# Residual as a fourth filter of the strip product, in a graph-attention and expert block on one core

## The reference

```python
out = 0
for k in range(3):                       # three graph filters
    r = einsum('mn,bmn,bmft->bnft', cheb[k], S, x)
    out = out + einsum('bnft,fo->bnot', r, Theta[k])
sg = relu(out)
tc = conv along t (3 taps, tw)(sg) + tb
res = einsum('bnft,of->bnot', x, rw) + rb
y = relu(res + tc)
y = layer_norm_over_t(y) * gamma + beta
```

## Time and profile before

| | |
|---|---|
| timed runs | 947.37, 949.14, 950.04 us (median 949.14) |
| span of the profiled execution | 943.2 us |
| median less span | 5.9 us |
| TensorE busy | 896.8 us, 95% |
| VectorE, ScalarE, GpSimd busy | 604.5, 426.2, 210.3 us |
| steady part | about 240 to 840 us |

### The profile page before, as it was taken

The page is one execution under the profiler, slowest core; times in us unless marked ns, Lnnn a source line. Parts: engine busy times, 40 slices in busy tenths (PEclk is TensorE's granted clock), DMA queues, the critical chain, the costliest instruction groups (busy, mean ns, idle before and its releaser), DMA issues.

```text
span 943.2 us, 19688 instructions
## 1 busy us (share of the span) xinstructions
PE 896.8 (95%) x8000; PEld 799.1 (85%) x8000; DVE 604.5 (64%) x1615; ACT 426.2 (45%) x781; POOL 210.3 (22%) x183
## 2 busy tenths in 40 slices
PE   4898879999999999999999999999999999999997
PEld 3687658998988998898988989888888898988997
DVE  6637967677775379654786458853787537764522
ACT  2534534831674336552464425652366424622442
POOL 2004101233301142112411124021331123122232
PEclk9999999999999999999999999999999999999998
DMA  6000400111011100210002010020001100020121
GB/s 233 2 1 1 171 23 2 57 62 35 13 39 57 35 24 13 73 35 23 24 14 82 24 35 23 25 72 31 27 13 52 55 2 24 30 77 24 38 66 34
DMA packets 36249, 39.26 MB, mean 42 GB/s; under 512 B 3392, under 2 KB 32576, under 8 KB 36160
## 3 DMA queue, kind: packets, MB, share of 16 engines
q1 hardware_dynamic: 36160, 38.01, 12.7%
HBM read 33.02 MB, written 4.98 MB: 40 GB/s over the span
## 4 chain that ended last, share of the span: by engine, by line
PE 85%; DVE 6%; DMA 4%; ACT 2%; issue 2%; POOL 1%; SPq 0%; POOLq 0%; DVEq 0%
PE ring L1355 9%; PE d_ps L521 5%; PE g_ps L521 5%; PE d_ps L522 4%; PE d_ps L523 4%; PE g_ps L523 4%; PE g_ps L522 4%; PE u_ps L522 4%; PE u_ps L521 4%; PE u_ps L523 4%; PE ring L1223 4%; PE num L1252 3%; PE ring L1338 3%; PE ring L1455 3%; PE ring L521 3%; PE ring L523 2%
## 5 line engine op out<-in xcount | busy, mean ns | idle before, releaser
L699 POOL TENSOR_TENSOR hl<-hb,hh 128x512 fp32r<-128x512 f32 x96 | 126.7, 1320 | 480.0 <-ACT hh L836 480.0
L836 ACT ACTIVATE hh<-hb 128x512 fp32r<-128x512 f32 x96 | 60.6, 632 | 181.8 <-DVE hb L1195 169.4
L521 PE MATMUL d_ps<-hh,down_h 128*128 128x256 f32 x384 | 114.9, 299 | 5.1 <-POOL hl L699 5.1
L521 PE MATMUL g_ps<-normed_h,gate_h 128*128 128x256 f32 x352 | 107.4, 305 | 3.5 <-DVE hb L1190 3.5
L1190 DVE TENSOR_TENSOR hb<-sl,u_ps 128x512 f32<-128x512 f32 x88 | 60.2, 684 | 77.2 <-PE u_ps L523 35.9
L522 PE MATMUL d_ps<-hl,down_h 128*128 128x256 f32 x384 | 107.7, 280 | 0.0
L523 PE MATMUL d_ps<-hh,down_l 128*128 128x256 f32 x384 | 107.7, 280 | 0.0
L522 PE MATMUL g_ps<-normed_l,gate_h 128*128 128x256 f32 x352 | 99.8, 283 | 0.0
L523 PE MATMUL g_ps<-normed_h,gate_l 128*128 128x256 f32 x352 | 99.8, 283 | 0.0
L522 PE MATMUL u_ps<-normed_l,up_h 128*128 128x256 f32 x352 | 99.5, 283 | 0.0
L521 PE MATMUL u_ps<-normed_h,up_h 128*128 128x256 f32 x352 | 99.4, 283 | 0.0
(11 more groups left out here) (413 smaller groups left out, 2092.5 us busy)
## 6 DMA issues: line engine op xcount, KB each, us to landing
weights_over_hidden<-weights_by_expert SPq DMA_DIRECT2D x128, 128.0 KB, 2.9
shared<-denominators_by_head SPq DMA_DIRECT2D x16, 256.0 KB
out_x<-kept SPq DMA_DIRECT2D x16, 256.0 KB, 2.2
x_s<-in_x SPq DMA_DIRECT2D x12, 256.0 KB, 3.6
raw_weights<-in_gateT SPq DMA_DIRECT2D x4, 384.0 KB, 6.6
raw_weights<-in_upT SPq DMA_DIRECT2D x4, 384.0 KB, 6.0
raw_weights<-in_down SPq DMA_DIRECT2D x4, 384.0 KB, 8.0
cheb_s<-in_cheb SPq DMA_DIRECT2D x3, 256.0 KB, 4.9
```

What stands on the lines that cost most here:

```text
L521: eng.matmul(ps, wh, xh, start=start, stop=False, **how)
L699: pool.tensor_tensor(hl[:, j % 2, :], hb, hh[:, j % 2, :].bitcast(F32), ALU.subtract).then_inc(*ffn_pool.mark(p, f"lo{j}"))
L836: act.activation(hh[:, j % 2, :], hb, ACT.Copy).then_inc(*ffn_act.mark(p, f"hi{j}"))
```

## The change

The weights of the residual become a fourth filter: `theta_s` gets 4 x 2 x 16 = 128 columns, and TensorE's filter products write whole banks. ScalarE now makes two copies from each of the four banks: the three filters to `y_s` as before, and the fourth to the rows in `kept`, in which it waits for the output store. The bank is free after the second copy. GpSimd then adds the bias to the rows in place. In tc0 and tc1 the bias product and the residual products are gone; TensorE does the temporal convolution alone, VectorE adds the rows to the bank in place, and ScalarE's relu waits for that. The load of `residual_s` and the preparation of `ones`, `bias_h` and `bias_hl` go.

```diff
-        theta_s = sb("theta_s", [P, 3, 2, T])
-        residual_s = sb("residual_s", [P, T, 8])
+        theta_s = sb("theta_s", [P, 4, 2, T])
...
-                READ_OUT[f"Y{b}_{j}"] = [(conv_act, f"y{b}{j}")]
+                READ_OUT[f"Y{b}_{j}"] = [(conv_act, f"r{b}{j}")]
...
+                if name in ("Y0", "Y1"):
+                    b = int(name[1])
+                    if p == 0 and not b:
+                        pool.wait_ge(prep_dve, 6)
+                    pool.wait_ge(conv_act.of(p), conv_act.at(p, f"r{b}3"))
+                    res = x1_at(p)[:, :, b, :].rearrange("p m (c s) -> p m c s", s=2 * T)
+                    pool.tensor_tensor(res, res, bias[:, :, :].rearrange("p t o -> p (t o)").unsqueeze(1).to_broadcast([P, 8, 2 * T]).unsqueeze(1).to_broadcast([P, 2, 8, 2 * T]),
+                                       ALU.add).then_inc(*conv_pool.mark(p, f"rb{b}"))
...
+                    if p >= 3:
+                        act.wait_ge(out_stored[p % 3], 32 * (p // 3))
                     for j, n in enumerate(banks_of(name)):
-                        act.activation(g.y_s[b].rearrange("p m c k s -> p (m c k) s")[:, :, 32 * j:32 * j + 32],
-                                       tile(p, n)[:, 0:384].rearrange("p (q s) -> p q s", s=32), ACT.Copy).then_inc(*conv_act.mark(p, f"y{b}{j}"))
+                        act.activation(g.y_s[b].rearrange("p m c k s -> p (m c) k s")[:, :, :, 32 * j:32 * j + 32],
+                                       tile(p, n)[:, :].rearrange("p (q k s) -> p q k s", k=4, s=32)[:, :, 0:3, :], ACT.Copy).then_inc(*conv_act.mark(p, f"y{b}{j}"))
+                        by_k = tile(p, n)[:, :].rearrange("p (m c k s) -> p m c k s", m=2, c=2, k=4)
+                        act.activation(x1_at(p)[:, :, b, :].rearrange("p m (c s) -> p m c s", c=2)[:, :, :, 32 * j:32 * j + 32], by_k[:, :, :, 3, :],
+                                       ACT.Copy).then_inc(*conv_act.mark(p, f"r{b}{j}"))
...
                 if name in ("tc0", "tc1"):
                     b = int(name[2])
-                    if p >= 3:
-                        act.wait_ge(out_stored[p % 3], 32 * (p // 3))
+                    act.wait_ge(conv_dve.of(p), conv_dve.at(p, f"res{b}"))
...
+                if name in ("tc0", "tc1"):
+                    b = int(name[2])
+                    dve.wait_ge(*filled_at(p, name))
+                    dve.wait_ge(conv_pool.of(p), conv_pool.at(p, f"rb{b}"))
+                    by_o = t[:, :].rearrange("p (m o t) -> p m o t", m=2, t=T)
+                    dve.tensor_tensor(by_o, by_o, x1_at(p)[:, :, b, :].rearrange("p m (t o) -> p m o t", o=T), ALU.add).then_inc(*cv.mark(p, f"res{b}"))
...
-                            last = pe.matmul(tile(p, n)[:, q * 96:(q + 1) * 96], g.xT[rows, b, c, m * P:(m + 1) * P],
+                            last = pe.matmul(tile(p, n)[:, q * P:(q + 1) * P], g.xT[rows, b, c, m * P:(m + 1) * P],
...
-                    pe.matmul(by_o, ones[:, :], bias_hl[:, :].unsqueeze(1).to_broadcast([P, 2, T]).unsqueeze(3).to_broadcast([P, 2, T, T]),
-                              start=True, stop=False, skip_group_check=True)
                     for m in range(2):
                         cols = slice(m * P, (m + 1) * P)
-                        for c in range(2):
-                            pe.matmul(by_o[:, m, :, 8 * c:8 * c + 8], g.xT[:, b, c, cols], residual_s[:, :, :], start=False, stop=False, skip_group_check=True)
-                        pe.matmul(by_o[:, m, :, 0:9], g.sg[:, b, 0, cols], tconv_s[:, :, 1:10], start=False, stop=False, skip_group_check=True)
+                        pe.matmul(by_o[:, m, :, 0:9], g.sg[:, b, 0, cols], tconv_s[:, :, 1:10], start=(m == 0), stop=False, skip_group_check=True)
                         last = pe.matmul(by_o[:, m, :, 7:16], g.sg[:, b, 1, cols], tconv_s[:, :, 0:9], start=False, stop=True, skip_group_check=True)
```

More of the change, by code:

```diff
@@ L217, with graph_attention_moe @@
 PLACE = {f: i for i, f in enumerate(FILLS)}
-def graph_attention_moe(nc, x, out, small, consts, cheb, theta, residual, tconv, vsT, bsT, wqkvT, woT, gateT, upT, down):
+def graph_attention_moe(nc, x, out, small, consts, cheb, theta, tconv, vsT, bsT, wqkvT, woT, gateT, upT, down):
     x_v = x.rearrange("(p b) (c n) f t -> p b n c (f t)", b=2, n=P)
@@ L240, in graph_attention_moe @@
         cheb_s = sb("cheb_s", [P, 3, 2, N])
[L241 to L242 removed]
+        theta_s = sb("theta_s", [P, 4, 2, T])
         tconv_s = sb("tconv_s", [P, T, 10])
[L244 to L246 removed]
+        bias = sb("bias", [P, 2, T])
         vs_s = sb("vs_s", [P, 2, N])
@@ L257, in graph_attention_moe @@
         down_h = sb("down_h", [P, CHUNKS, N], F32R)
-        ones = sb("ones", [P, P], F32R)
         over = sb("weights_over_hidden", [P, 2, 512])
@@ L578, in _ @@
             sp.dma_start(theta_s[:, :, :, :], theta).then_inc(load["blocks"], 16)
-            sp.dma_start(residual_s[:, :, :], residual).then_inc(load["blocks"], 16)
             sp.dma_start(tconv_s[:, :, :], tconv).then_inc(load["blocks"], 16)
@@ L722, in front @@
                 if t is not None:
-                    act_reads = name in ("xT0", "xT1", "lr", "o0", "o1", "tc0", "tc1", "xl0", "xl1", "xn0", "xn1", "kt", "q0", "q1", "k0", "k1", "v0", "v1")
+                    act_reads = name in ("xT0", "xT1", "lr", "o0", "o1", "xl0", "xl1", "xn0", "xn1", "kt", "q0", "q1", "k0", "k1", "v0", "v1")
                     if act_reads:
@@ L726, in front @@
                 if name == "M" and p == 0:
-                    act.wait_ge(prep_dve, 6)
-                    act.wait_ge(prep_pool, 6)
-                    act.activation(bias_h[:, :], bias[:, :], ACT.Copy).then_inc(prep_act, 1)
-                    act.activation(bias_hl[64:65, :], bias[64:65, :], ACT.Copy).then_inc(prep_act, 1)
+                    act.wait_ge(prep_pool, 2)
                 if name in ("xT0", "xT1"):
@@ L851, in prepare @@
                 dve.tensor_tensor(router[:, :, 1, :], small_at("router").rearrange("p (k e) -> p k e", k=2), router[:, :, 0, :].bitcast(F32), ALU.subtract).then_inc(prep_dve, 1)
-                dve.tensor_tensor(bias[:, :], small_at("tb"), small_at("rb"), ALU.add).then_inc(prep_dve, 1)
-                dve.tensor_scalar(ones[:, :], ident, 0.0, 1.0, ALU.mult, ALU.add).then_inc(prep_dve, 1)
+                dve.tensor_tensor(bias[:, :, :], small_at("tb").unsqueeze(1).to_broadcast([P, 2, T]), small_at("rb").unsqueeze(1).to_broadcast([P, 2, T]),
+                                  ALU.add).then_inc(prep_dve, 1)
             def split(i):
@@ L965, in front @@
                     dve.wait_ge(load["rest"], 16)
-                    dve.wait_ge(prep_act, 3)
-                    dve.wait_ge(prep_dve, 6)
-                    dve.tensor_tensor(bias_hl[96:97, :], bias[96:97, :], bias_h[96:97, :].bitcast(F32), ALU.subtract).then_inc(prep_dve, 1)
                     dve.wait_ge(load["graph"], 96)
@@ L1563 @@
     consts = _np.concatenate([c[n].astype(f32) for n in CONST], axis=1)
-    theta = _np.zeros((8, T, 3, 2, T), f32)
-    residual = _np.zeros((8, T, T, 8), f32)
+    theta = _np.zeros((8, T, 4, 2, T), f32)
     tconv = _np.zeros((8, T, T, 10), f32)
     for t in range(8):
-        theta[t, :, :, t % 2, :] = a["L0_conv_Theta"].transpose(1, 0, 2)
-        residual[t, :, :, t] = a["L0_conv_rw"].T
+        theta[t, :, 0:3, t % 2, :] = a["L0_conv_Theta"].transpose(1, 0, 2)
+        theta[t, :, 3, t % 2, :] = a["L0_conv_rw"].T
         tconv[t, :, :, t:t + 3] = a["L0_conv_tw"][:, :, 0, ::-1].transpose(1, 0, 2)
-    theta, residual, tconv = (v.reshape((P,) + v.shape[2:]) for v in (theta, residual, tconv))
+    theta, tconv = (v.reshape((P,) + v.shape[2:]) for v in (theta, tconv))
     given = {
-        "x": a["x"], "small": small, "consts": consts, "cheb": a["L0_conv_cheb"], "theta": theta, "residual": residual, "tconv": tconv,
+        "x": a["x"], "small": small, "consts": consts, "cheb": a["L0_conv_cheb"], "theta": theta, "tconv": tconv,
         "vsT": a["L0_conv_V_s"].T, "bsT": a["L0_conv_b_s"][0].T,
```

19 lines of the change are left out of this document (6 added, 13 removed).

## The result

The changed kernel takes **937.17 us** (median of four runs, 933.71 to 938.39) beside 949.59 for the kernel before, run between them (947.37 to 950.96): a ratio of 0.9869, 95% interval 0.9843 to 0.9896, so it is 12.4 us or 1.3% faster (10 to 15 us). I had forecast 4.9. The direction was right and the range held the time, in part by luck, but the gain is two and a half times the forecast, and the sum behind it has to be taken apart.

A forecast was written before the change was run, and what follows sets the result against it. TensorE, busy 95% of the span, was taken to bound the kernel. Five steady pairs at -0.85 us (-4.2) and the opening (-0.7) gave -4.9, so 949.14 would become 944.3 us; range 935.5 to 952.

The forecast's parts named there:

- Where is this paid?: Places where TensorE feels ScalarE's added copies and the wider products: Y0 0.5 us, Y1 0.35 us a pair.
- 0.5 us behind Y0: Y0: 0.1 wider products plus 0.68 copies less 0.27 slack delay the tanh and the routing weights' copy, per pair.
- 0.35 behind Y1: Y1: ring banks come free later, 0.25 for st1's transposes and 0.1 for o0, per pair.
- a term put at nothing: Behind Y0: the routing weights' DMA chain and TensorE's 0.96 us wait at its end, with only new delay charged.
- tc1 waiting for the relu of o1: At tc1: it would begin at 434.02, just as that relu ends, a new stall of 0.25 us.
- The spacing: ScalarE's four added copies per filter tile start 0.17 us after their neighbours by overlapping: 0.68 us a tile.
- The rivals with full-length copies: Y0 and Y1: each added copy costs its full 0.28 us, 1.1 a tile; 948.0 us, chance 0.22.
- the gate on ScalarE: Y0 and Y1: old copies lose their overlap too, 3.1 us a tile in place of 1.64; 953.6 us, chance 0.13.
- the queue of VectorE ahead of V11 and wo0: After tc: additions delay VectorE's later work; 0.6 us a pair lost, of which 0.25 is tc1's wait for the relu.
- forecast -0.85: Steady part, each pair: -1.7 left of the removed products, +0.5 at Y0, +0.35 at Y1.
- Opening: Pairs 0 to 2, without feed-forward work to hide behind: gains and delays sum to -0.7 us, give or take 1.5.
- The median of the runs lies 5.9 us above the span, which stays: Baseline: median of the runs 5.9 us above the profiled span of 943.2; the gap stays, so 949.14 less 4.9.

The follow-up runs named there:

- experiment 8: Changed kernel without VectorE's addition, ScalarE's residual copies and GpSimd's bias additions; filter products still 128 columns wide, residual and bias missing: 929.98 us, ratio 0.9795.
- experiments 3: Changed kernel without VectorE's addition; the relu reads the bank straight after the convolution, copies and GpSimd's bias additions stay: 929.85 us, ratio 0.9801.
- Experiment 11: Changed kernel with GpSimd writing residual and bias in the bank's order, so VectorE's addition reads 512 numbers in a row: 936.99 us, ratio 0.9863.
- experiment 2: Kernel before with 128 empty waits more at the start of TensorE's stream, moving its instruction loads: 954.93 us, ratio 1.0062.
- experiment 6: Changed kernel with 48 empty waits before TensorE's wait for its first load, on a semaphore up at once: 938.10 us, ratio 0.9889.
- second profiles: Kernel before and changed kernel each run and profiled once more, no edit: 947.64 us (span 945.9) and 936.71 us (span 934.9).
- experiments 1: Kernel before with bias and residual products left out of both temporal convolutions, nothing put in their place: 929.87 us, ratio 0.9794.
- 7: Changed kernel with the old scheme (bias and residual products in tc, three filters, no additions) in pairs 0 and 1: 934.42 us, ratio 0.9846.
- 12: Changed kernel with the old scheme in pairs 0 and 1 and the residual in the bank's order in pairs 2 to 7: 933.59 us, ratio 0.9831.
- 4: Changed kernel with 64 empty waits more at the start of TensorE's stream: 943.15 us, ratio 0.9942.
- 5: Kernel before with 48 empty waits before TensorE's wait for its first load, on a semaphore up at once: 948.78 us, ratio 0.9997.

## Why the prediction was right or wrong

**The step that failed.** The sum missed 7.5 of 12.4 us. Two terms of it were wrong. The first is the answer to "Where is this paid?": I charged the copies and wider products with 0.5 us behind Y0 and 0.35 behind Y1, 0.85 a pair, and TensorE felt 0.25 to 0.3, so nearly 3 us too much in five pairs. The second is a term put at nothing: I took the write of the routing weights, and TensorE's wait at its far end, as given, and looked only at what the change would add to them. In place of that its meetings with instruction loads fell from five to two, 2.3 to 3.9 us. Most of the rest lies at the end of the program (about 1 us) and in how executions differ. (The parts do not add up to 7.5 exactly: the meetings cost other amounts in other executions.) The first term is a mistake about the change; the second is luck, since no part of the edit aims at it.

**What bounds the kernel.** Right: a product removed gave back 94% of its time (2.16 of 2.31 us). I had charged 0.25 us of it for tc1 waiting for the relu of o1. The timeline of after has no such wait, and tc0 to the next step takes 433.56 - 431.66 = 1.90 us where I had 2.2 and before had 4.27 (start, duration, what):

```profile
431.66 0.41 PE L1373 MATMUL ring<-tconv_s,filters 128*128 128x144 f32 x2
431.86 0.60 ACT L775 ACTIVATE filters<-ring 128x512 f32<-128x512 f32 x1 [4.58 <-PE ring L1361]
...
432.64 0.45 PE L1373 MATMUL ring<-tconv_s,filters 128*128 128x144 f32 x2
432.84 2.08 DVE L981 TENSOR_TENSOR ring<-ring,kept 128x512 f32<-128x512 f32 x2 [5.47 <-PE ring L1374]
...
433.56 0.37 PE L517 MATMUL d_ps<-hh,down_h 128*128 128x256 f32 x1
...
433.92 0.60 ACT L779 ACTIVATE kept<-ring 128x512 f32<-128x512 f32 x1 [1.46 <-DVE ring L981]
434.82 1.45 DVE L1005 TENSOR_REDUCE row_sums<-kept 128x32 f32<-128x512 f32 x2
434.95 0.60 ACT L779 ACTIVATE kept<-ring 128x512 f32<-128x512 f32 x1 [0.44 <-DVE ring L981]
```

The convolutions follow each other without a gap; the relu of o1 ends at 432.46, just ahead of tc1. One check in the prediction does not come out: its pieces, 0.41 + 0.31 + 4 x 0.44, make 2.48 and not 2.31 us; the 2.31 from the starts is the better figure.

**ScalarE's copies.** The spacing was right to the hundredth. In after eight copies run from 378.75 to 381.07, 2.32 us against 1.64, so 0.17 for each added one:

```profile
378.75 0.49 ACT L741 ACTIVATE filters<-ring 128x384 f32<-128x384 f32 x1 [1.44 <-issue]
379.14 0.27 ACT L744 ACTIVATE kept<-ring 128x128 f32<-128x128 f32 x1
379.30 0.50 ACT L741 ACTIVATE filters<-ring 128x384 f32<-128x384 f32 x1
...
380.97 0.21 ACT L749 ACTIVATE conv_small<-conv_small 16x32 f32<-16x32 f32 x1
```

The rivals with full-length copies and with the gate on ScalarE fell with it. The Trainium skill, "VectorE: DVE Perf Modes", section "The TRN2 errata", gives, as an estimate worked out from its cycles, 0.25 for each exposed copy; the trace does not agree, 0.17.

What failed is the step from there to TensorE. *Y0:* I had 0.5 with the wider products. The tanh starts 2.22 us behind the first copy in place of 1.91, so 0.31, and the clean short stretches grow by the same: 40.9 to 41.18. It starts 0.10 before the last copy has ended. Of the growth, the wider products make about 0.1 (experiment 8). *Y1:* I had 0.35; experiments 3 and 8 show 0 in the long stretch. The transposes of st1 start 1.01 us behind the start of V10's products before and after; the 0.20 us put down there to ScalarE, and again in after, does not grow with the copies, so the bank was not what came last.

For both, 0.85 forecast, 0.25 to 0.3 measured: 0.6 us a pair too much, the largest wrong term of the steady sum.

**VectorE's addition.** I took 0.62 to 0.69 us from VectorE operations that read in a row; this one reads its second operand with a stride of 16 numbers and takes 1.04. Experiment 11 shows that the order is the cause. A rule that bears on it is in the Trainium skill, "Advanced Engine Details and Errata", section "SBUF Cachelines": consecutive accesses that leave a 16-byte line pay a penalty; the trace agrees, 1.04 against 0.70 us. I named the wrong place as well: not the queue of VectorE ahead of V11 and wo0, but the bank that S11 awaits behind addition and relu:

```profile
435.69 0.66 PE L1229 MATMUL ring<-shared 32*128 32x256 f32 x5 [0.46 <-ACT kept L779]
```

The weight loads of the same products stand idle for 0.63 us there, for 0.27 in experiment 11, and without a wait in experiment 3, which has no addition. It is the only gap of that size which TensorE has in this stretch of after and not in that of experiment 3.

Price 0.60 us a pair where I had 0.35. From before to after the long stretch fell by 1.65, so 0.66 of 2.31 was lost where I had 0.6, of which 0.25 was a wait of tc1 that did not come. Two wrong places gave nearly the right sum, which is luck.

**The steady part without meetings.** Clean turns are 40.9 + 69.2 = 110.1 before (experiment 2) and 41.18 + 67.55 = 108.73 after (experiment 6): -1.35 us, forecast -0.85. From Y1 of pair 7 to the last instruction it is 2.6 us less (943.2 - 755.5 = 187.6, 934.8 - 749.8 = 185.0; 2.5 in the second profiles), of which a clean turn explains 1.65. Over five short stretches, four long ones and this end it is 5 x 0.25 - 4 x 1.65 - 2.6 = -7.9 us where I had -4.2.

**What was not in the sum: the meetings.** In the nine stretches from Y0 of pair 3 to Y1 of pair 7 the kernel before lost 487.1 - (5 x 40.95 + 4 x 69.2) = 5.6 us to five. The changed kernel lost 479.8 - 476.5 (the same nine in experiment 6) = 3.3 us to two. That makes -2.3 us. The second profiles give 6.2 and 2.3, so -3.9. My row was there: VectorE's wait of 1.49 us for the weights by DMA, and I wrote of the chain that starts at comb only what would be added to it. That the same write took 1.59 us outside the steady part, against 2.83 here, was in the trace of before, and unasked. I also wrote that the other pairs repeat pair 4 within 0.1 us; the short stretches of before run from 41.91 to 42.31, and that spread was a sign.

**Opening.** I had -0.7. In the profiled executions the time to Y0 of pair 3 changes by +1.6 and +0.45, while the medians leave 12.4 - 7.9 - 2.3 = 2.2 us of gain for it, or 0.6 with the meetings of the second profiles. What may blur it is the granted clock. The page's rows, in tenths, before and after:

```profile
PEclk9999999999999999999999999999999999999998
...
PEclk9999799999999999999999999999999999999999
```

A stretch at the lower level (1.2 of 2.4 GHz, granted clock 0.50) of 6.8 us stands in after, at a place where before has none. Experiment 11 had one of 10.2, among others:

```profile
92.90:99.70 6.80, 5.76 (x25) 4.25 (x25) 4.53 (x10) 4.15 (x10) 3.07 (x3) 0.50 0.00 0
...
118.90:129.10 10.20, 9.32 (x50) 6.54 (x46) 6.20 (x10) 4.35 (x7) 0.00 (x0) 0.50 0.70 242
```

All such stretches lie in the opening (none starts later than 172 us) and in the last microseconds; between, the clock is at the upper level. Before Y0 of pair 3 they add up to 10.2 and 13.6 us in the two profiles of before, and to 17.0 in both of after. In four profiles with the changed steps (after twice, experiments 6 and 11) 17.0, 17.0, 34.1 and 37.5 us of them go with 270.0, 270.4, 276.1 and 276.3 us to Y0 of pair 3, some 0.32 us for each. By this estimate the 6.8 and 3.4 us that after has more cost it 2.2 and 1.1, and the opening itself gains 0.6 us in both pairs of profiles, near my -0.7.

Over all 142 runs of the study (least squares, one constant for each kernel) a mean clock lower by 0.001 goes with 0.58 us. Brought to a clock of 0.990 by that, before is 948.5, after 936.9, experiments 1 and 8 are 927.8 and 927.5, 3 is 931.1, 6 is 935.4, 7 is 934.0, 11 is 933.8 and 12 is 932.0. In this reckoning the change is: products gone -20.8 (meetings within), wider products -0.3, copies and bias additions +3.7, the addition +5.7, sum -11.7. The stretches give the last two only some 1 and 3 us in the steady part; the rest would be paid in the opening. For the copies that rests on the correction alone: the medians of experiments 8 and 3, 929.98 and 929.85, show nothing for them. That the clock is the cause and not only a companion is argued, not shown; no run held it fixed.

**The baseline.** "The median of the runs lies 5.9 us above the span, which stays": only 1.8 of it lies around the span, in every run. The other 4.1 were luck of the execution that was profiled. (Over all its 61 executions the kernel before has a median of 948.7, after has 936.7 over five, 12.0 less.) That did no harm to a difference, but it should have told me that one execution says little on the opening.

## What to carry to other kernels

Price a removed product at its full time, and a delay on a helper engine at what its *reader* feels: here 0.7 us of copies cost TensorE at most 0.3 at one place and nothing at the other. An operation's duration carries over only with the order in which it reads. Before forecasting a change of half a percent, look at whether the same transfer takes the same time in every round of the loop; a length of program changed by a few instructions can move what it meets by more than the change is worth, in either direction, so compare clean rounds with clean rounds.

## What the runs showed of the hardware

- A 16 KB load of TensorE's instructions in flight beside a 32 KB write lengthens the write from 1.6 us to between 2.4 and 3.5. The loads moved when TensorE's stream alone was lengthened (experiments 2, 4 to 6). The Trainium skill, "Advanced Engine Details and Errata", section "ISA Cache", says that such a line holds 256 instructions; the trace agrees: 64 loads for 16,000 matmuls and weight loads and some hundred waits. In the kernel before the loads come at the same phase of each turn, five meetings in a row; with 36 instructions fewer a turn they drift, and two turns of five hold a meeting.
- An empty wait instruction costs TensorE 0.10 to 0.12 us (experiments 2 and 4).
- VectorE, 128x512 with a bank as first operand and as output: 1.04 us with the second operand at a stride of 16 numbers, 0.70 in a row.
- Executions of one program spread over 8 us (the kernel before, 945.4 to 953.3), while the stretches of the steady part agree within 0.1 us from one to the next, and within 0.7 where they hold a meeting.
